# Last cross attention: the output product in three rounded products, and one unit's normalisation on ScalarE

## The reference, cut to what matters

```python
# L1 cross attention: x [32,112,256], context [32,375,192], 8 heads of 64
q = (layernorm(x) @ Wq);  k = context @ Wk;  v = context @ Wv
attn = softmax(q k^T * 64**-0.5)            # 8 heads x 112 x 375
out = (attn @ v)                            # 112 x 512
x = x + out @ Wo + bo                       # Wo is 512 x 256: the "out product"
# L1 ffn: rows quantised in blocks of 32 to a 6-bit grid, then one 256x256 product
x = x + dequant(quant(layernorm(x))) @ dequant(quant(W)).T + bias
```

## Time and profile before

| | us |
|---|---|
| median of 3 runs (range) | 1942.99 (1941.95 to 1943.06) |
| the profiled execution | 1940.72 |
| its span in the trace | 1938.9 |
| share of the span busy: PE, DVE, ACT, POOL | 96%, 78%, 66%, 49% |
| granted TensorE clock, mean | 0.982 of full |

### The profile page before, as it was taken

One profiled execution on the slowest core, in us unless ns is written; L12 is line 12 of the kernel. 1 busy time (PEld: TensorE's weight loads), 2 busy tenths in 40 slices (PEclk: granted clock), 3 DMA queues, 4 the chain that ended last, 5 costly groups with the idle time before them and its releaser, 6 DMA issues.

```text
span 1938.9 us, 61565 instructions
## 1 busy us (share of the span) xinstructions
PE 1862.4 (96%) x20887; PEld 1635.4 (84%) x20887; DVE 1504.0 (78%) x3442; ACT 1271.2 (66%) x2721; POOL 945.7 (49%) x1612
## 2 busy tenths in 40 slices
PE   7999999999899999879999999969999999999996
PEld 5888888888678888679999999958888888888885
DVE  6787888878478878756666666667999999999986
ACT  2555555555477777557777777747777777777773
POOL 4556555665256667640000000047676767677751
PEclk9999999999899999889999999979999999999998
DMA  8222233222051111265555555431111111111100
GB/s 239 91 89 89 89 107 100 89 89 64 11 178 31 38 37 36 62 242 195 203 197 189 195 205 196 162 84 56 36 41 35 34 41 32 41 31 42 33 16 10
DMA packets 116595, 182.05 MB, mean 94 GB/s; under 512 B 10850, under 2 KB 94562, under 8 KB 116066
## 3 DMA queue, kind: packets, MB, share of 16 engines
q1 hardware_dynamic: 110386, 166.51, 26.8%
q0 software_dynamic: 6144, 14.69, 2.6%
HBM read 127.68 MB, written 53.48 MB: 93 GB/s over the span
## 4 chain that ended last, share of the span: by engine, by line
PE 91%; DVE 3%; ACT 2%; DMA 1%; issue 1%; POOL 1%; ACTq 0%; SPq 0%; DVEq 0%; POOLq 0%
PE ps_quad L1535 11%; PE ps_proj L182 9%; PE ps_out L1555 9%; PE ps_quad L182 6%; PE ps_quad L549 5%; PE ps_turned L108 4%; PE ps_quad L102 4%; PE ps_out L114 4%; PE ps_out L557 3%; PE ps_proj L2029 3%; PE ps_turned L182 3%; PE ps_quad L2009 3%; PE ps_proj L641 2%; PE ps_turned L768 2%; PE ps_out L1251 2%; PE ps_turned L535 2%
## 5 line engine op out<-in xcount | busy, mean ns | idle before, releaser
L1535 PE MATMUL ps_quad<-e_xT,w 128*128 128x128 f32 x2016 | 235.3, 275 | 1.8 <-DVE e_xT L1491 1.8
L1535 PEld LDWEIGHTS ps_quad<-e_xT,w 128*128 128x128 f32 x2016 | 230.4, 192 | 2.3 <-DVE e_xT L1491 2.3
L369 ACT ACTIVATE a_probsT<-ps_quad 125x1792 f32<-125x1792 f32 x96 | 159.9, 1665 | 98.2 <-PE ps_quad L549 98.2
L1677 POOL TENSOR_TENSOR c_held<-minus_half 1x1 f32<-1x1 f32 x32 | 8.9, 279 | 407.0 <-DMA slots<-e_y 404.5
L1438 ACT ACTIVATE e_act_T<-ps_quad,fc_b 128x128 f32<-128x128 f32 x504 | 136.8, 383 | 91.4 <-PE ps_quad L1535 91.2
L134 ACT ACTIVATE c_probs<-ps_quad,c_negmax 112x375 f32<-112x375 f32 x256 | 143.6, 570 | 38.6 <-DVE c_negmax L119 38.6
L126 DVE TENSOR_SCALAR c_probs<-c_probs,c_recip 112x375 f32<-112x375 f32 x256 | 163.1, 678 | 4.6
L1555 PE MATMUL ps_out<-e_w2H,e_aH 128*128 128x256 f32 x504 | 149.0, 296 | 6.7 <-DVE e_w2L L1479 6.6
L1479 DVE TENSOR_TENSOR e_w2L<-w,e_w2H 128x1024 fp32r<-128x1024 f32 x126 | 150.5, 1236 | 0.0
L434 DVE TENSOR_REDUCE a_negmax<-ps_turned 112x2 f32<-112x750 f32 x128 | 120.1, 939 | 34.0 <-PE ps_turned L535 33.8
L1555 PE MATMUL ps_out<-e_w2L,e_aH 128*128 128x256 f32 x504 | 143.1, 284 | 0.0
(11 more groups left out here) (364 smaller groups left out, 6005.8 us busy)
## 6 DMA issues: line engine op xcount, KB each, us to landing
w<-in_fc_t SPq DMA_DIRECT2D x71, 1024.0 KB, 4.9
slots<-a_zeros SPq DMA_DIRECT2D x60, 512.0 KB, 4.9
a_cT<-in_ctx_t SPq DMA_DIRECT2D x32, 375.0 KB, 3.5
c_cT<-in_ctx_t SPq DMA_DIRECT2D x32, 375.0 KB, 3.2
e_xg<-slots SPq DMA_DIRECT2D x63, 128.0 KB, 3.8
slots<-e_y SPq DMA_DIRECT2D x63, 128.0 KB, 1.8
out<-c_fo SPq DMA_DIRECT2D x32, 112.0 KB, 1.9
residual<-in_x SPq DMA_DIRECT2D x1, 2912.0 KB, 19.9
```

The source lines that it names most:

```text
L369: act.activation(probsT[:, 2 * i:2 * i + 2, :, :].rearrange("p c r x -> p r c x"), quad[0:KC, :, 0:2 * HALF].rearrange("p r (c x) -> p r c ...
L1535: last = pe.matmul(hidden[par][:, c // 4, (c % 4) * TILE:(c % 4 + 1) * TILE], mem["w1"][:, par, k, c * 128:(c + 1) * 128], xT[par][:, k, : ...
```

## The change

The out product takes halves. At the start of the stage ACT rounds the weights `wo` to `woH`, and DVE subtracts to get `woL`. In each step ACT writes `oH` (rounded, the same instruction as the copy to `oT` before), DVE computes `oL = ps_out - oH` between the second and the third part of the quantisation, and PE multiplies with 12 matmuls of halves in place of 4 of float32. DVE no longer scales unit 3: it leaves only the reciprocal there, and ACT scales the two heads, between the exponential of unit 1 and the spread of unit 2. Semaphore values follow.

```diff
+    def dve_reciprocal(self, dve, u):
+        dve.reciprocal(self.recip[:, u, :], self.sums[:, u, :]).then_inc(self.recip_ready, 1)
+    def act_normalise(self, act, u):
+        for j in range(2):
+            p = self.probs[u][:, j, :]
+            last = act.activation(p, p, ACT.Copy, scale=self.recip[:, u, j:j + 1])
+        last.then_inc(self.scaled, 1)
...
-        oT = sb("oT", [128, 4, T])
+        oH, oL = (sb(n, [128, 4, T], F32R) for n in ("oH", "oL"))
...   ACT, at step -2
+                        act.wait_ge(weights_in, 16 * len(loads))
+                        act.activation(woH[:, :, :], wo[:, :, :], ACT.Copy).then_inc(wo_high, 1)
...   ACT, after the exponential of unit 1
+                    if exists(b - 1):
+                        act.wait_ge(core.recip_ready, 4 * b)
+                        core.act_normalise(act, 3)
...
-                        act.activation(oT[:, :, :].rearrange("p k t -> p (k t)"), psum["out"][:, 0:4 * T], ACT.Copy).then_inc(o_ready, 1)
+                        act.activation(oH[:, :, :].rearrange("p k t -> p (k t)"), psum["out"][:, 0:4 * T], ACT.Copy).then_inc(o_high, 1)
...   DVE, before the maximum of unit 0
+                    if isinstance(b, int) and b == -1:
+                        dve.wait_ge(wo_high, 1)
+                        dve.tensor_tensor(woL[:, :, :], wo[:, :, :], woH[:, :, :], ALU.subtract).then_inc(wo_split, 1)
...
-                        core.dve_normalise(dve, 3, 4 * b + 4)
+                        core.dve_reciprocal(dve, 3)
...   DVE, between quantise(b - 1, 1) and quantise(b - 1, 2)
+                    if exists(b):
+                        dve.wait_ge(o_high, b + 1)
+                        wait(dve, op_mm, b)
+                        dve.tensor_tensor(oL[:, :, :].rearrange("p k t -> p (k t)"), psum["out"][:, 0:4 * T],
+                                          oH[:, :, :].rearrange("p k t -> p (k t)"), ALU.subtract).then_inc(o_ready, 1)
...   PE
-                    for k in range(4):
-                        last = pe.matmul(to[0:T, 0:D], oT[:, k, :], wo[:, k, :], start=(k == 0), stop=(k == 3))
-                    last.then_inc(op_mm, 1)
+                    chain(pe, to[0:T, 0:D], [pair for k in range(4) for pair in split_terms((oH[:, k, :], oL[:, k, :]), (woH[:, k, :], woL[:, k, :]))])\
+                        .then_inc(op_mm, 1)
...   PE, before the transposition of unit 3
-                        pe.wait_ge(core.probs_ready, 4 * b)
+                        pe.wait_ge(core.scaled, b)
```

More of the change, by code:

```diff
@@ L95, in __init__ @@
         self.recip_ready, self.probs_ready, self.turned_ready = sem("recip_ready"), sem("probs_ready"), sem("turned_ready")
+        self.scaled = sem("scaled")
         self.spread_act, self.values_ready = sem("spread_act"), sem("values_ready")
@@ L1598, in cross_last @@
         mx = {n: sb(f"mx_{n}", [T, D // MX if n in ("scale", "inv") else D]) for n in ("scale", "inv", "t", "magic", "q", "d")}
+        woH, woL = (sb(n, [128, 4, D], F32R) for n in ("woH", "woL"))
+        wo_high, wo_split, o_high = sem("wo_high"), sem("wo_split"), sem("o_high")
         weights_in, c_in = sem("weights_in"), [sem("c_in0"), sem("c_in1")]
@@ L2101, in step @@
                         pe.wait_ge(o_ready, b - 1)
+                        if isinstance(b, int) and b == 2:
+                            pe.wait_ge(wo_split, 1)
                         if exists(b + 1):
@@ L2124, in step @@
                     if exists(b - 1):
-                        pe.wait_ge(core.probs_ready, 4 * b - 1)
+                        pe.wait_ge(core.probs_ready, 3 * b)
                         if exists(b - 1):
@@ L2249, in step @@
                     if exists(b):
-                        pe.wait_ge(core.probs_ready, 4 * b + 2)
+                        pe.wait_ge(core.probs_ready, 3 * b + 2)
                         if exists(b + 1):
@@ L2276, in step @@
                     if exists(b):
-                        pe.wait_ge(core.probs_ready, 4 * b + 1)
+                        pe.wait_ge(core.probs_ready, 3 * b + 1)
                         if exists(b):
```

## The result

The changed kernel takes 1966.31 us (median of 4 runs, 1964.4 to 1966.78) and the kernel before, timed beside it, 1942.47 (4 runs, 1941.13 to 1943.06). The ratio is 1.0123, with a 95% interval from 1.0112 to 1.0135: slower by 23.8 us, where 16.5 were forecast (1959.5). Timed again with the second set of experiments: 1964.25 against 1942.63, ratio 1.0108 (1.0092 to 1.0125).

The account below looks back on a forecast made before the run. PE was taken to bound at 19.58 us a period; 1.48 added to a loop with slack 0.64 and 1.09 gives 15.9, plus 1.15 and -0.6 at the ends: 16.5 slower, 1959.5 us, range of 8 in 10 1946 to 1968.

Parts of the forecast that it names:

- the second loop: Loop through DVE, ACT and PE, 18.94 or 18.49 in two alternating kinds of period: 0.64 and 1.09 short of PE's 19.58.
- The low half costs 0.54: DVE's new subtraction between the maxima of units 3 and 0 adds 0.54 to the loop (0.33 to 0.62).
- ACT's pair costs 0.94: ACT's two scaling passes for unit 3, before the spread of unit 2, add 0.94 to the loop (0.86 to 1.14).
- Sum in the loop: Additions of 1.48 make periods 20.42 and 19.97 instead of 19.58, 15.9 us over 27 periods.
- DVE's scaling of unit 3 is worth nothing on the path: Removing 1.67 from DVE after unit 1's maximum only lengthens its wait for PE's scores of unit 3.
- The later `xd` costs nothing on top: Later `xd` delays POOL's low half and PE's transposition of `xd` (up to 0.2), both less than the loop's delay.
- The out product saves 0.40: Twelve matmuls of halves replace PE's 1.91 float32 group, saving 0.40 a batch; PE's own period becomes 19.18.
- The ends: Outside the 27 periods: +1.15 for making `woL` before the first maximum, -0.6 for the rest, uncertainty 2.
- PE idle before the transposition of unit 3: Sign expected in the profile after: PE idle there once a period, released by ACT's spread; its absence would refute the forecast.
- PE alone: Rival: PE alone sets the period, 0.40 saved in each of 32 batches, less 1.15: 1931.3; chance 0.08.
- only ACT's part: Rival: DVE's stretch between maxima does not grow, the loop gains only ACT's 0.94: 1945; chance 0.08.
- POOL did not hinder the new subtraction: Answers the rival that POOL hold-ups of about 1.0 a period cost more: 1986, or 1971 in one kind; chance 0.10.

Follow-up runs that it names:

- Experiment 2: Kernel before with only ACT scaling unit 3 (DVE leaves the reciprocal), out product still float32: 1947.07 us, ratio 1.0024.
- experiment 3: Changed kernel with ACT's scaling of unit 3 moved before the exponential of unit 0, reciprocals of units 2 and 3 joined: 1944.45 us, ratio 1.0009.
- experiment 1: Changed kernel with DVE scaling unit 3 again, keeping the out product in halves and the low half on DVE: 1954.63 us, ratio 1.0067.
- experiment 6: Changed kernel with ACT's scaling before unit 0's exponential, DVE's mixing before unit 3's maximum, and `woL` made one step earlier: 1936.32 us, ratio 0.9967.
- experiments 5: Changed kernel with DVE's mixing of the gathered rows moved from behind to before the maximum of unit 3: 1948.46 us, ratio 1.0034.
- experiment 4: Kernel before, unchanged, run once more for the scatter of its profile: 1941.55 us, ratio 0.9999.
- 8: Changed kernel, run once more for a second profile: 1964.25 us, ratio 1.0108 to the kernel before.
- experiment 7: Kernel before with ACT scaling unit 3 before unit 0's exponential and DVE's mixing moved, out product still float32: 1943.19 us, ratio 1.0001.

## Why the prediction was right, and where it was off

*PE bounds before, and the second loop is 0.64 and 1.09 behind it.* Right. Experiment 2 puts about a microsecond into this loop alone, and the two kinds of period answer with what exceeds their slack, within 0.03.

*The low half costs 0.54.* Too small, the larger of two terms that were mis-sized. By itself it costs that: 0.54 from its start to its successor's (1509.81 to 1510.35), its record being 0.62, and 0.624 to 0.626 in all 32. The Trainium skill ("SBUF — State Buffer", Who interferes with whom) lets such an operation, with one input in PSUM, run beside GpSimd unhindered. The low half does not test that: wherever it overlaps an instruction of POOL, that is one of the gathers (27 of 32). The row that agrees is the one that the prediction named: the operation of the same form at 1526.74 (an addition, not a subtraction) took 0.41 inside POOL's 2.15. But before the low half DVE stands still for 0.19, put down to its own previous operation and not to ACT's high half, which had been there since 1509.44. The two operations around it are 1.16 apart (1509.19 to 1510.35). In the kernel before, the first of them is this row of DVE's timeline, and the second stands at 1518.59 in the earlier trace rows, 0.46 later; so the price is 0.70.

```profile
1514.51 0.41 DVE L169 TENSOR_SCALAR c_xn<-residual,c_norm_moments,c_norm_rstd 112x256 f32 x1 [0.41 <-DVE c_xq L169]
...
1518.13 0.42 DVE L1311 TENSOR_TENSOR c_mx_q<-c_mx_q,c_mx_magic 112x256 f32<-112x256 f32 x1
```

The first of these two rows shows that such idle time, put down to the engine's own previous operation, was there to be seen before. The stretch between maxima grew accordingly, 13.14 to 13.80 and 12.69 to 13.39.

It is not the waits as such. The idle time stands in front of all 24 low halves of the hardware loop and of none of the three in the straight code ahead of it, which have the same waits. There, in the changed kernel, the low half starts 0.47 after its predecessor like any link of the chain, and the stretch grew by 0.53 alone (12.69 to 13.22):

```profile
1347.39 0.43 DVE L1321 TENSOR_TENSOR c_mx_q<-c_mx_q,c_mx_magic 112x256 f32<-112x256 f32 x1
1347.86 0.62 DVE L2002 TENSOR_TENSOR c_oL<-ps_out,c_oH 128x448 fp32r<-128x448 f32 x1
```

In the loop the value waited for (`b + 1`) depends on the counter, and DVE's sequencer (DVEq) records one arithmetic operation on the line of that wait, 24 times, and none in straight code. In the chain of experiment 3, where the idle time is the same:

```profile
1522.98 0.44 DVE c_mx_q L1321
...
1523.45 0.04 DVEq L1997
...
1523.60 0.10 DVE c_oL L1999
```

It starts only when the predecessor has ended, since the chain's own wait for that result stands in front of it. The output row at 1519.29 in the changed kernel has three waits too, but none for DVE's own result, and starts before its predecessor's record ends. The prediction reckoned the instruction and left out the bookkeeping of the hardware loop in front of it. That this is where the 0.16 go is read from the traces; no run took the arithmetic away.

*ACT's pair costs 0.94.* Nearly: it is 1.00 from the first start to the spread's (1518.27 to 1519.27), and the way from exponential to spread grew from 2.24 to 3.21, so by 0.97. The estimate of 1.00 by the Trainium skill ("ScalarE: Activation LUTs", What ACT_TABLE_LOAD costs) was the better one; I had taken the exponential's 0.47, and two of those are short by 0.06.

*Sum in the loop.* Right in form. With 0.66 and 0.70 for the low half and 0.97 for the pair the two kinds are 20.57 and 20.16 (measured 20.57 and 20.14); with the three periods in straight code at 19.94, 27 periods add 12 x 0.99 + 12 x 0.56 + 3 x 0.36 = 19.7 in place of 15.9 (measured 19.55). This is where 3.7 of the missing 7 us are.

*DVE's scaling of unit 3 is worth nothing on the path.* True from the side from which it was asked: experiment 2 removes it and the stretch does not shrink. Wrong as a statement on the change: with the low half on DVE and the scaling too (experiment 1), DVE's list takes 20.33 in every second period. Without the removal the low half costs 12 us in the 27 periods. The two edits are not additive either: 12.2 and 3.4 in 27 periods make 15.6, together they make 19.55, because in experiment 1 it is another loop that ends last.

*The later `xd` costs nothing on top.* Right in the changed kernel, where PE idles before the transposition of unit 3. In experiments 1 and 3, where that loop does not end last, it does cost. In experiment 3 PE's run from the transposition of `xd` is late by some 0.2 a period; the cost had been covered.

*The out product saves 0.40.* It saves 0.31 in the chain (1.91 to 1.60, experiment 6), and in the changed kernel none of that is seen. The twelve products have 1.50 from their first start to that of the next product (1514.69 to 1516.19), near the 1.44 reckoned. But the 1.91 from which the prediction took it holds about 0.1 beside the products: the same float32 product, from its first start to that of the next one, has 1.81 (1523.03 to 1524.84).

*The ends.* `woL` cost 1.10 (the record at 1297.37 to the maximum at 1298.47), of which 0.9 reach the first maximum; the drain and the tail came to +0.5 in place of -0.6, and the fill to nothing. Within the uncertainty of 2 that I gave.

*PE idle before the transposition of unit 3.* Right (0.50, from ACT's spread), and DVE idle before the maximum of unit 3, forecast as well over 0.85, is 1.97 to 2.09. The rivals fall: PE alone is what experiment 6 is, not the change; only ACT's part would need a stretch between maxima that does not grow, and it grew by 0.66 and 0.70; and POOL did not hinder the new subtraction, which never took more than 0.626.

What is left, 1942.47 + 19.6 + 1.4 = 1963.5 against 1966.31 and 1964.25, is of the size by which the earlier stages differ between executions. So the mechanism held, and the size was short by the 0.16 a period, by the ends, and by something outside the stage that no run explains.

## What to carry to other kernels

An engine that is busy for the whole of a stage may be followed by a loop through three other engines that is only 3% shorter, and moving work off the busy one is worth nothing until that loop is summed, start to start, and each addition is put on its side of the wait that closes it. The same work cost 22 us or gave back 6 in one set of runs, depending on whether it stood before or behind a wait that was there anyway: look first for an idle time of the same engine in the same period. And sum each engine's own list as a loop as well, idle time in front of its instructions and lengthened neighbours included; a removal that is off the path today may be what pays for an addition.

## What the runs showed of the hardware

In the hardware loop an operation of DVE that waits for a value computed from the counter, behind a wait for DVE's own previous result, was preceded by 0.19 of idle time though what it waited for had long come (4.6 over 24 of them), so it cost 0.70; in straight code the same operation with the same waits cost 0.54. An ACT pass over 112x375 with its factor per row from memory cost 0.50 from start to start.

The mean of DVE's scaling over 112x375 was 605, 632, 687 or 748 ns in four kernels (changed, experiment 6, before, experiment 1) in which it is the same instruction. The likely cause is what POOL does at that moment, and moving one operation shifts the meetings of the others; which of them met was not counted.

The three stages ahead of the changed one, whose code none of these kernels touches, ended up to 5.8 us later than in the first profile of the kernel before (experiment 3), and up to 0.8 earlier (experiment 6). Part of this is the granted TensorE clock at the border between the first two stages. The chain there in the changed kernel, then in the kernel before:

```profile
501.36 1.96 PE ps_quad L559 x28
503.31 1.98 PE ps_out L658 x4
505.29 1.98 PE ps_quad L559 x27
```

```profile
499.97 1.10 PE ps_quad L549 x28
502.89 1.16 PE ps_quad L549 x32
505.80 1.14 PE ps_quad L549 x28
```

From 501.3 to 507.3 the granted clock is 0.50 of full in the changed kernel (1.2 GHz) and full in the kernel before (2.4 GHz): the same groups take nearly 2.0 and 1.1, and the border costs 2.0 us more. PE had been waiting for DVE just before in both kernels: from 494 to 500 it is busy for 4.49 us in the changed one and for 4.18 in the one before, at full clock. Over 480 to 520 us the mean granted clock was 0.98 of full in the profiles of the kernel before and of experiments 5 and 6, 0.99 in experiment 4, 0.96 in 1, 0.94 in 8, and 0.91 in the changed kernel and in experiments 2, 3 and 7. The clock there does not settle the whole: experiment 7 has 0.91 too, and its three stages end only 1.3 later. The two profiles of the changed kernel differ (0.91 and 0.94), a scaling at the end of the third stage starts at 1271.9 and 1269.4 in them and at 1266.8 and 1267.6 in those of the kernel before. So it seems a matter of the execution rather than of the change, but ten profiles do not settle whether a kernel makes it likelier. What starts it stays open.

Not tried: the low half on another engine or behind `xd`, its place in front of the chain's own wait, and the pair's place varied without the reciprocals joined.
